# Five banks instead of four for the picked node table, and 12, 12, 5 and 7 picked columns of 25

## The reference

```python
# L0: an MLP makes a 16x16 matrix of each edge; message = x[src] @ matrix
h = relu(edge_attr @ W1 + b1); weights = (h @ W2 + b2).reshape(-1, 16, 16)
out = segment_sum(einsum('ei,eio->eo', x[src], weights), dst) + x @ root
# L1: two graph convolutions (16 -> 32 -> 16) with normalised edge weights
msg = (x @ W.T)[src] * (dis[src] * w * dis[dst]); out = segment_sum(msg, dst)
# L2: 230 relations, messages mapped into a ball (norm, tanh), weighted mean
msg = exp_map(einsum('ei,eio->eo', h_tan[src], rel_weight[etype]) + rel_emb[etype])
# L3: 90 relations (30 bases), message times an attention term
msg = einsum('ei,eio->eo', h[src], W_rel[rel_type]) * e; out = segment_sum(msg, dst)
# after each layer: x = layernorm(x + layer(x))
```

## Time and profile before

| | |
|---|---|
| median of 3 runs | 16053.67 us (16048.67 to 16054.34) |
| the profiled execution's span | 16080.2 us |
| PE, busy | 12414.4 us, 77% |
| DVE, busy | 12672.3 us, 79% |
| ACT, busy | 8008.6 us, 50% |
| POOL, busy | 11959.0 us, 74% |

### The profile page before, as it was taken

How to read it: one execution, slowest core, us unless ns; L and a number is a source line. 1 busy time by engine, 2 the same in 40 slices (tenths; PEclk the granted TensorE clock), 3 DMA queues, 4 the chain that set the end, 5 groups by cost and what they waited for, 6 DMA issues and landing times.

```text
span 16080.2 us, 197886 instructions
## 1 busy us (share of the span) xinstructions
PE 12414.4 (77%) x62964; PEld 11204.4 (70%) x62964; DVE 12672.3 (79%) x13275; ACT 8008.6 (50%) x6941; POOL 11959.0 (74%) x12266
## 2 busy tenths in 40 slices
PE   6777777777599999599999488888888377777774
PEld 5555555555599998599999377777777376766764
DVE  7777777777577777477777589899989599999996
ACT  1111111111466666466666377777777255555552
POOL 6777777777777777677777677777777577777776
PEclk8888888888799999799999688898888577777776
DMA  1111111111122221122221122222222222222221
GB/s 37 28 27 27 28 28 27 28 28 26 33 40 39 40 39 37 28 40 39 40 39 38 37 48 50 50 51 50 50 47 48 44 61 62 63 60 63 61 62 37
DMA packets 811074, 675.53 MB, mean 42 GB/s; under 512 B 420924, under 2 KB 729500, under 8 KB 810500
## 3 DMA queue, kind: packets, MB, share of 16 engines
q1 hardware_dynamic: 419012, 545.90, 11.4%
q0 software_dynamic: 392000, 128.94, 9.3%
HBM read 507.78 MB, written 166.09 MB: 42 GB/s over the span
## 4 chain that ended last, share of the span: by engine, by line
POOL 57%; issue 20%; DVE 8%; DVEq 8%; PE 6%; DMA 1%; ACT 0%; POOLq 0%; SPq 0%; ACTq 0%
POOL deep L637 54%; DVE big L1292 6%; PE PS L855 5%; DVEq L1040 4%; DVEq L1297 3%; POOL deep L646 3%; DVE sml L1561 0%; DVEq L1232 0%; DVE acc L1229 0%; DMA wgt<-in_edge_weight 0%; DVEq L1286 0%; DVE sml L1553 0%; DVE acc L1566 0%; DVE sml L1554 0%; DVE sml L1558 0%
## 5 line engine op out<-in xcount | busy, mean ns | idle before, releaser
L637 POOL DMA_INDIRECT deep<-table,idx x11750 | 11475.0, 977 | 3824.8 <-issue 3579.0
L797 PE MATMUL PS<-tparts,hot 125*128 125x400 f32 x22000 | 4163.7, 350 | 482.7 <-DVE big L1451 305.4
L797 PEld LDWEIGHTS PS<-tparts,hot 125*128 125x128 f32 x22000 | 4078.7, 192 | 567.4 <-DVE big L1451 387.1
L1292 DVE TENSOR_TENSOR big<-PS,deep 128x768 f32<-128x768 f32 (+4 forms) x2750 | 2984.7, 1085 | 1082.2 <-DMA deep<-table,idx 515.5
L855 PE MATMUL PS<-tparts,rhot 125*128 125x426 f32 (+1 forms) x9000 | 2302.2, 428 | 527.7 <-DVE big L1292 293.8
L855 PEld LDWEIGHTS PS<-tparts,rhot 125*128 125x128 f32 x9000 | 2177.8, 246 | 616.3 <-DVE big L1292 320.7
L944 ACT ACTIVATE hot<-deep,ones_col 128x1536 fp32r<-128x1536 bf16 x1000 | 1447.6, 1472 | 1464.7 <-PE PS L797 1424.8
L754 PE MATMUL PS<-w0b_sb,big 128*128 128x256 f32 x6250 | 1826.1, 437 | 428.4 <-DVE big L1292 390.1
L754 PEld LDWEIGHTS PS<-w0b_sb,big 128*128 128x128 f32 x6250 | 1342.2, 222 | 933.7 <-DVE big L1292 475.0
L869 PE MATMUL PS<-wx,hot 115*128 115x272 f32 x12500 | 1726.1, 293 | 311.1 <-DVE big L1292 311.1
L1275 DVE TENSOR_REDUCE acc<-big 128x64 f32<-128x1024 f32 (+2 forms) x1875 | 1940.6, 1035 | 18.3
(11 more groups left out here) (281 smaller groups left out, 9713.7 us busy)
## 6 DMA issues: line engine op xcount, KB each, us to landing
wide<-edge_types SPq DMA_DIRECT2D x250, 800.0 KB, 6.1
deep<-table,idx POOLq DMA_INDIRECT x11750, 2.4
wide<-pick_codes SPq DMA_DIRECT2D x250, 352.0 KB, 3.5
running<-msg SPq DMA_DIRECT2D x250, 212.5 KB, 2.1
running<-msg SPq DMA_DIRECT2D x250, 200.0 KB, 2.0
running<-msg SPq DMA_DIRECT2D x125, 400.0 KB, 2.5
wide<-in_edge_attr SPq DMA_DIRECT2D x125, 200.0 KB, 2.5
tabo<-pick_codes SPq DMA_DIRECT2D x125, 160.0 KB, 4.6
```

The source lines that it names most:

```text
L637: pool.indirect_dma_start(g[:, j, 0:GW[l]], None, tab_dram[l][:, :], bass.IndirectOffsetOnAxis(ap=idx[:, s, j:j + 1], axis=0)).then_inc(ga ...
L797: last = pe.matmul(o, poneh[0:NQ, m, c], tparts[0:NQ, k, m * JC:m * JC + JC], start=m == 0 and k == 0, stop=m == BK - 1 and k == 1)
L1292: dve.tensor_tensor(products(j), matv(l, j, n), xs, ALU.mult).then_inc(mats_free, 1)
```

## The change

The fold goes from 4 banks of 25 rows to 5 banks of 20. PK becomes 0, 12, 12, 5 and 7, so a chunk gathers 13, 13, 20 and 18 columns where it gathered 14, 14, 21 and 20. A picked column now takes 10 matmuls of 320 columns (340 in pass 4) where it took 8 of 400 (426). The groups of passes 1 and 2 are 3, 3, 3 and 3 columns; pass 3 has pick groups of 3 and 2, pass 4 of 2, 2, 2 and 1, in other PSUM banks. ACT makes five distances where it made four. The picks' one-hots of passes 3 and 4 move from the tile `rhot` into `hot`, behind the types' one-hots; `deep` grows by 640 elements so that five banks of distances fit, and the distances of pass 4 lie in the whole of `late`.

```diff
-    PK = [0, 11, 11, 4, 5]
+    PK = [0, 12, 12, 5, 7]
...
-    BK, JR = 4, NJ // 4
+    BK, JR = 5, NJ // 5
...
-    GRP = [(0, 3), (3, 3), (6, 3), (9, 2)]
-    RGRP = [[], [], [], [(0, 4)], [(0, 3), (3, 2)]]
+    GRP = [(0, 3), (3, 3), (6, 3), (9, 3)]
+    RGRP = [[], [], [], [(0, 3), (3, 2)], [(0, 2), (2, 2), (4, 2), (6, 1)]]
...
-    BANKS = [[(2 * (k % 2), 2) for k in range(8)], None, None, [(4, 4)] + [(4 * (i % 2), 4) for i in range(6)] + [(3, 1)],
-             [(0, 3), (3, 2), (5, 2), (0, 2), (2, 2), (4, 2), (6, 2), (3, 2), (7, 1)]]
+    BANKS = [[(2 * (k % 2), 2) for k in range(8)], None, None, [(0, 3), (4, 2)] + [(4 * (i % 2), 4) for i in range(6)] + [(3, 1)],
+             [(4, 2), (6, 2), (0, 2), (2, 1)] + [((2 * i + 4) % 8, 2) for i in range(6)] + [(0, 1)]]
...
-        deep = sb("deep", [P, 3200 + S * CH * 17])
+        DIST = max(CH * P, BK * NPK * P // 2)
+        deep = sb("deep", [P, DIST + S * CH * 17])
...
-        hot = sb("hot", [P, 2 * CH * P], F32R)
+        HALVES = [0, 0, 0, 2, 1]
+        hot = sb("hot", [P, max(BK * NPK * P, max(HALVES[l] * CH * P + BK * PK[l] * P for l in (3, 4)))], F32R)
...
-        rhot = sb("rhot", [P, BK, RPK * P], F32R)
-        rdist = Z.bitcast(BF16)[:, 0:RPK * BK * P].rearrange("p (m n) -> p m n", m=BK)
+        rdists = [(Z if l == 3 else late).bitcast(BF16)[:, 0:PK[l] * BK * P].rearrange("p (m n) -> p m n", m=BK) for l in (3, 4)]
...
+                rdist, rhot, oneh = rdists[l - 3], pick_hots(l), type_hots(l)
...
-                    act.activation(rdist[:, m, 0:w], rcodes[:, HOME[s], 0:w], ACT.Abs, bias=negbank[:, m:m + 1])
+                    act.activation(rdist[:, m, :], rcodes[:, HOME[s], 0:w], ACT.Abs, bias=negbank[:, m:m + 1])
```

More of the change, by code:

```diff
@@ L211, in build_gnn, with type_hots, pick_hots @@
         sml = sb("sml", [P, 12, CH])
-        hot = sb("hot", [P, 2 * CH * P], F32R)
+        HALVES = [0, 0, 0, 2, 1]
+        hot = sb("hot", [P, max(BK * NPK * P, max(HALVES[l] * CH * P + BK * PK[l] * P for l in (3, 4)))], F32R)
         poneh = hot[:, 0:BK * NPK * P].rearrange("p (m n) -> p m n", m=BK)
-        oneh = hot[:, :].rearrange("p (h n) -> p h n", h=2)
+        def type_hots(l):
+            return hot[:, 0:HALVES[l] * CH * P].rearrange("p (h n) -> p h n", h=HALVES[l])
+        def pick_hots(l):
+            c0 = HALVES[l] * CH * P
+            return hot[:, c0:c0 + BK * PK[l] * P].rearrange("p (m n) -> p m n", m=BK)
         dst_now = wide[:, 3 * CH * P // 2 - TILES:3 * CH * P // 2]
@@ L261, in build_gnn @@
         dist = big1[:, :].bitcast(BF16).rearrange("p (h n) -> p h n", h=2)
-        pdist = big1[:, 0:BK * NPK * P // 2].bitcast(BF16).rearrange("p (m n) -> p m n", m=BK)
+        pdist = deep[:, 0:BK * NPK * P // 2].bitcast(BF16).rearrange("p (m n) -> p m n", m=BK)
         X = sb("X", [P, NF])
@@ L854, in relation_pass @@
                                     for k in range(2):
-                                        last = pe.matmul(o, rhot[0:NQ, m, c], tparts[0:NQ, k, m * pc:m * pc + pc],
+                                        last = pe.matmul(o, pick_hots(l)[0:NQ, m, c], tparts[0:NQ, k, m * pc:m * pc + pc],
                                                          start=m == 0 and k == 0, stop=m == BK - 1 and k == 1)
@@ L868, in relation_pass @@
                                     rhs = tab[0:K, k, h, :] if l == 3 else tab[0:K, k, :]
-                                    last = pe.matmul(o, oneh[0:K, h, (t0 + u) * P:(t0 + u) * P + P], rhs,
+                                    last = pe.matmul(o, type_hots(l)[0:K, h, (t0 + u) * P:(t0 + u) * P + P], rhs,
                                                      start=z == 0, stop=z == len(parts) - 1)
@@ L993, in one_hots @@
                 act.wait_ge(mats, it * (S * ng) + (o0 + ng * s - ng + NPG[l]))
-                act.activation(rhot[:, :, 0:w], rdist[:, :, 0:w], ACT.Relu, bias=ones_col[:, 0:1], scale=-1.0).then_inc(poneh_ready, 1)
+                act.activation(rhot, rdist, ACT.Relu, bias=ones_col[:, 0:1], scale=-1.0).then_inc(poneh_ready, 1)
                 for b, (t0, n) in enumerate(HALF):
```

4 lines of the change are left out of this document (2 added, 2 removed).

## The result

The changed kernel takes 16273.26 us (median of 4 runs, 16261.26 to 16281.66) where the kernel before, run beside it, takes 16054.01 (4 runs, 16048.67 to 16062.07): a ratio of 1.0138, 95% interval 1.0125 to 1.0150. It is slower by 219 us; 216 were forecast. The profiled executions have spans of 16279.4 and 16080.2, 199 us apart: the first lies 6 us above its median and the second 26.

What follows compares the result with a forecast made beforehand. The prediction took POOL to pace passes 1 and 2, with PE 93% busy, and DVE chiefly to pace passes 3 and 4. Its terms, 54 + 45 + 109 + 8 = +216 us, gave 16270 us, range 16090 to 16430.

Steps and rivals of the forecast that it cites:

- Passes 1 and 2: PE and its loop with DVE take over from POOL; each chunk grows 0.21 us, +54 us in both passes.
- DVE's tail: Passes 1 and 2: DVE from a chunk's last pick product to the next chunk's first, 7.54 us becoming 7.59.
- rival (a): PE's overhead goes with columns, 136 ns per 320-column matmul; passes 1 and 2 gain 142 us, total 15990; 7%.
- The loop: Passes 1 and 2: PE's and DVE's mutual waiting, 8.93 us plus two groups of 30 matmuls at 9.10, 18.03 a chunk.
- the outer turn: Passes 1 and 2: 0.1 us a chunk added for the outer loop's turn in one chunk of five.
- Pass 3: DVE paces; selector to first matrix product grows 0.38 us a chunk, waits for picks unchanged; +45 us.
- Pass 4: DVE picks more elements in four groups, +1.31 us a chunk, less the vanished waits; chunk 26.6 us, +109 us.
- Starts: First chunks of passes 3 and 4 get longer by ACT's new work, +8 us.
- (b): Passes 3 and 4: PE's clock falls after more idle time, picks arrive late; +433 us, total 16487; 13%.
- (c): Passes 1 and 2 at their low bound, pass 3 without waits; +58 us, total 16112; 12%.
- (d): Passes 1 to 4: saved gathers pay as POOL's chain share suggests, 1.25 us each; -783 us, total 15270; 2%.

Runs made afterwards that it cites:

- e3b: Changed kernel with one of the ten matmuls of each picked column left out in passes 1 and 2; 16027.29 us.
- e5: Kernel before with one gather a chunk left out in passes 1 to 4, nothing picked in its place; 15734.88 us.
- e4b: Changed kernel with ACT's relu of the picks' one-hots moved ahead of the types' distances; 16453.53 us, 1.0251 of the kernel before.
- e1b: Changed kernel with pass 4 put back to 5 picked columns in groups of 3 and 2; 16137.77 us.

## Why the prediction was right

**Passes 1 and 2 (+54; measured +52.7).** Right in the sum and in the main cause, that PE with its matmuls takes over from POOL; not in how the sum is made up. A turn of pass 1 in the changed kernel, DVE and then PE, against the earlier trace rows:

```profile
5400.74 1.16 DVE L1462 TENSOR_TENSOR big<-PS,sel 128x960 f32<-128x960 f32 x1 [2.18 <-PE PS L807]
...
5408.35 1.16 DVE L1462 TENSOR_TENSOR big<-PS,sel 128x960 f32<-128x960 f32 x1 [0.19 <-issue]
...
5395.70 24.55 PE L807 MATMUL PS<-tparts,hot 125*128 125x320 f32 x164
```

DVE's tail is 7.61 us, forecast 7.59. PE runs on without a break through 164 matmuls: (24.55 - 0.31) / 163 = 149 ns each, as the overhead of 15 to 16 ns an instruction said; 136, on which rival (a) rested, is refuted. The loop, 18.03, is too long by 0.1: with e3b's 17.03 it would be 17.92, and the median chunk is 17.94. PE's own stream of 17.9 sets it in most chunks and not the loop, which the forecast had in front; PE waited for DVE 47 times, 17.7 us in the whole pass. The forecast's 0.1 for the outer turn is there (mean 18.04).

The forecast has every chunk grow by 0.21, from 17.93 to 18.14. But 17.93 is the window of a pass divided by 125 and mixes its start, its fast chunks and its steady ones. The selectors of chunks 2, 21 and 125 show two paces in the kernel before (first three rows) where the changed one has one:

```profile
4219.14 0.44 DVE L1254 TENSOR_TENSOR sel<-PS,rsel 128x275 f32<-128x275 f32 x1 [0.25 <-issue]
4543.60 0.45 DVE L1254 TENSOR_TENSOR sel<-PS,rsel 128x275 f32<-128x275 f32 x1 [0.76 <-issue]
6417.28 0.45 DVE L1254 TENSOR_TENSOR sel<-PS,rsel 128x275 f32<-128x275 f32 x1 [0.25 <-issue]
```

```profile
4216.87 0.41 DVE L1265 TENSOR_TENSOR sel<-PS,rsel 128x240 f32<-128x240 f32 x1 [0.25 <-issue]
4559.71 0.41 DVE L1265 TENSOR_TENSOR sel<-PS,rsel 128x240 f32<-128x240 f32 x1 [0.76 <-issue]
6435.97 0.41 DVE L1265 TENSOR_TENSOR sel<-PS,rsel 128x240 f32<-128x240 f32 x1 [0.25 <-issue]
```

Before, the first 19 distances average 17.08 us (the first fifteen 16.8, near the 16.7 of e5) and the other 104 18.02. POOL starts gathering 36 us before DVE's second chunk and has issued the gathers of two chunks by then, so it has a lead of one chunk, which is used up at about the twentieth; of DVE's waits for gathers 5.7 us fall in the first stretch and 97.9 in the second. After, it is 18.04 in both. So in pass 1 18 of the 25 us are lost while POOL's lead lasted, 4 in the first chunk (2.3 forecast), and only 3 in the remaining 104 chunks, where 14 gathers before and 120 matmuls now cost the same within 0.03 us; the end of the pass, forecast at -1.4, is unchanged. In pass 2 it is 17, 5 and 6. A growth of 0.21 in every chunk was too much (0.03 and 0.06 are steady); that the total agrees within 2 us is owed to the lost lead, which the forecast doesn't have, and is luck.

By the Trainium skill, "TensorE: Matmul & The Clock Gate", section "Back-to-back issue gap", 320 columns should be 136 ns apart at the full clock and 267 at the lower one; the section calls this the gap of an isolated matmul. The second agrees with pass 3, where 19 such matmuls take 5.13 us at a granted clock of 0.50, 270 each; the first is 13 ns short here.

**Pass 3 (+45; measured +40.9).** The DVE work that was forecast is there, but half of the +40.9 is something else. A chunk start of the changed kernel, against the earlier trace rows:

```profile
10542.16 0.32 DVE L1265 TENSOR_TENSOR sel<-iota_f,rsel 128x100 f32<-128x100 f32 x1 [0.20 <-issue]
10542.67 1.16 DVE L1303 TENSOR_TENSOR big<-PS,sel 128x960 f32<-128x960 f32 x1 [0.19 <-issue]
10544.52 0.82 DVE L1303 TENSOR_TENSOR big<-PS,sel 128x640 f32<-128x640 f32 x1 [0.69 <-PE PS L865]
...
10547.22 1.28 DVE L1303 TENSOR_TENSOR big<-PS,deep 128x1088 f32<-128x1088 f32 x1
```

From selector to first matrix product there are 5.06 us; without the wait of 0.69 where 0.17 is the usual gap, 4.54, which is the forecast. The wait has moved to the second pick group. The forecast took the wait as unchanged. Over the pass it looks so: DVE idles before its products for 53.7 + 49.7 + 32.0 = 135 us (first chunk left out; PE's two lines and its own gaps) where it was 86.1 and 37 of gaps, but it has 381 such gaps of at least 0.17 where it had 272; less those, 71 and 76. Yet the mean hides two kinds of chunk. Chunks 84 to 95, from 11389.45 to 11737.53, take 29.01 us each and the other 111 take 27.27, and in the twelve PE does what it does all through pass 3 of e4b:

```profile
11408.78 7.61 PE L865 MATMUL PS<-tparts,hot 125*128 125x320 f32 x50
11420.49 12.07 PE L879 MATMUL PS<-wx,hot 115*128 115x272 f32 x80 [4.10 <-DVE big L1303]
...
11420.49:11424.20 3.71, 3.71 (x17) 3.71 (x18) 2.70 (x3) 3.42 (x3) 2.59 (x3) 0.55 0.82 248
```

The picks run early at the full clock, PE stands, and the matrix matmuls begin at the lower clock. This costs 12 x 1.73 = 21 us. e3b, with the same code in pass 3, has no such stretch and a pass of 3438.6, +21 on the kernel before; e1b has eight such chunks. In e3b DVE idles for 57.4 + 25.6 + 30.6 = 114 us in 366 gaps, 51 less those, where it was 76. So without such a stretch the waits do fall, by 0.2 us a chunk, and the pass grows by 21 us and not by 45; the rest of the agreement is chance. What starts and ends such a stretch isn't shown. The 50 picks take 10.13 us (10.1 forecast), with 19 at 0.27 where 22 had been put. PE's start after its last matrix product was put at about 3 us and is 2.3: ACT's one-hots are ready earlier than worked out.

**Pass 4 (+109; measured +110.9 with its start).** Selector, first product and first matrix product of one chunk, and PE's picks, against the earlier trace rows:

```profile
14013.96 0.31 DVE L1265 TENSOR_TENSOR sel<-iota_f,rsel 128x140 f32<-128x140 f32 x1 [0.19 <-issue]
14014.55 0.87 DVE L1303 TENSOR_TENSOR big<-PS,sel 128x680 f32<-128x680 f32 x1 [0.28 <-issue]
...
14020.92 1.21 DVE L1303 TENSOR_TENSOR big<-PS,deep 128x1024 f32<-128x1024 f32 x1
...
14004.61 12.75 PE L865 MATMUL PS<-tparts,hot 125*128 125x340 f32 x70 [4.21 <-DVE big L1303]
```

6.96 us where 6.99 was forecast, 12.75 for the 70 picks where "about 13" was, and a chunk of 26.62 for 26.6. e1b shows the other half: with five columns a chunk that doesn't wait takes about 24.4.

**Starts (+8; measured 7).** First chunk and end of passes 3 and 4 together grew by 1 and 6 us: the pass less 123 mean chunks is 82.9 where it was 81.7, and 81.1 where it was 75.

**The rivals.** (b), picks late by a lower clock, did not happen at its size (136 and 235 us): DVE waits for the second pick group for 53.5 us in pass 3 and hardly in pass 4. But the clock does cost time: 21 us in the twelve chunks of pass 3, and 1.5 us a chunk in e4b, by another way than was thought (early picks and banks that aren't free, not late one-hots). (c) would need PE under 146 ns. (d) is refuted by e5 as well: one gather less a chunk is worth 317 us when nothing replaces it, not 640.

**Where the forecast's sum was lucky.** Added over the profiled spans it was +216 for +199; the medians are 219 apart. Pass 4 is right for its reasons. In passes 1 and 2 POOL's lead at the start of a pass makes up for a steady growth that is a tenth to a third of the forecast's, and in pass 3 twelve slow chunks make up for waits that shrank. The direction and what limits each pass are shown; the agreement within 4 us says nothing more.

## What to carry to other kernels

Moving work off an engine that leads the chain pays only up to the next limit, and that limit must be worked out for each stage: here about 0 to 1.15 us of the 1.28 that a gather costs POOL. Look at the chunks in order before dividing a pass by their number: a lead of the slowest engine at the start can hide in the mean, and an episode of a few slow chunks too. Take the two halves of such a change apart: the finer fold was good (128 us a pass with 12 columns), the counts were one too high in the passes that pick, and the fold with 11, 11, 4 and 6 columns is 0.5% faster than the kernel before. When an engine is made ready earlier, look at the buffer that it needs next; time won in front of a full buffer can come back as a lower clock.

## What the runs showed of the hardware

- PE's clock can fall where it costs most: after a stand of 4.40 us the granted clock is 0.55 for the next 3.70 us, and about 17 matmuls run where 28 would at 129 ns each. The same happens after a stand of 4.10 us in the changed kernel. Where the stands were shorter, 0.85 and 0.71 us ahead of e4b's picks at 10514.94, the picks ran at a granted clock of 1.00.
- A matmul of this kind brings 15 to 16 ns over its columns at 272, 320 and 400 columns alike, so cutting 8 x 400 into 10 x 320 costs about 22 ns (8 x 183.1 against 10 x 148.7).
- In one group of runs PE paused for 0.3 to 1.8 us between matmuls with no releaser in the profile, and ratios between kernels shifted: 1.0493, 1.0394 and 1.0560 for three kernels that stand at 1.0054, 0.9965 and 1.0251 otherwise.
